# Four message-passing layers in one program: stage borders, edge attributes and the encoder-decoder data flow rearranged

## The reference

```python
h = jnp.maximum(_layernorm(x, axis=-1), 0.0)
x = x + _L0_gnn_ref(h, edge_index, ...)      # normalised sums over sources, then one matmul
h = jnp.maximum(_layernorm(x, axis=-1), 0.0)
x = x + _L1_gnn_ref(h, ..., edge_type_8)     # one of 8 matrices per edge, sums over targets
h = jnp.maximum(_layernorm(x, axis=-1), 0.0)
x = x + _L2_gnn_ref(h, edge_index, ...)      # encoder 128->128->64, decoder 64->128->128
h = jnp.maximum(_layernorm(x, axis=-1), 0.0)
x = x + _L3_gnn_ref(h, edge_attr_32, ...)    # attention over edges, needs efeats @ a_e
```

## Time and profile before

| | us |
|---|---|
| median of 2 runs | 7244.42 (7242.15 to 7246.7) |
| the profiled execution | 7248.66 |
| its span, first to last instruction | 7246.9 |

### The profile page before, as it was taken

How to read it: one execution, slowest core, us unless ns; L and a number is a source line. 1 busy time by engine, 2 the same in 40 slices (tenths; PEclk the granted TensorE clock), 3 DMA queues, 4 the chain that set the end, 5 groups by cost and what they waited for, 6 DMA issues and landing times. The chain is left out here.

```text
span 7246.9 us, 107353 instructions
## 1 busy us (share of the span) xinstructions
PE 3460.2 (48%) x18429; PEld 2590.8 (36%) x18429; DVE 4887.1 (67%) x19215; ACT 2860.8 (39%) x7124; POOL 4935.2 (68%) x4572
## 2 busy tenths in 40 slices
PE   7655366556668888820027776001884333333000
PEld 1111255546667777720015555001663222222000
DVE  7999688876778888878867776223773455555544
ACT  0366211118863333346656665000331355554222
POOL 0377578884557777777767750777887677775677
PEclk9755599998989999965568888555997555555555
DMA  7488678779973333357779997223995333332443
GB/s 298 150 293 293 186 136 144 142 120 323 340 224 97 97 94 97 94 150 196 197 261 378 374 348 236 52 52 109 349 342 181 100 102 102 102 102 82 135 135 113
DMA packets 1168584, 1327.05 MB, mean 183 GB/s; under 512 B 231276, under 2 KB 968790, under 8 KB 1157939
## 3 DMA queue, kind: packets, MB, share of 16 engines
q1 hardware_dynamic: 961680, 1002.76, 42.6%
q0 software_dynamic: 206768, 323.00, 18.7%
HBM read 706.30 MB, written 646.54 MB: 187 GB/s over the span
## 5 line engine op out<-in xcount | busy, mean ns | idle before, releaser
L1807 PE MATMUL ps<-dense,w 128*128 128x256 f32 x3136 | 731.3, 386 | 146.1 <-DVE dense L1537 145.2
L555 POOL DMA_INDIRECT t_src<-tot,sidx x392 | 621.5, 1585 | 182.6 <-issue 90.2
L1807 PEld LDWEIGHTS ps<-dense,w 128*128 128x128 f32 x3136 | 581.6, 190 | 263.6 <-DVE dense L1537 162.3
L715 POOL DMA_INDIRECT dense<-t_y,ends_i x392 | 372.9, 951 | 329.4 <-ACTq L453 210.2
L1731 PE MATMUL ps<-oneh_c,oneh_p 128*128 128x395 f16 x1568 | 458.8, 430 | 279.4 <-DVE oneh_c L890 270.3
L785 ACT ACTIVATE estd<-emv,epsc 128x2 f32<-128x2 f32 (+1 forms) x588 | 174.1, 296 | 943.8 <-DVE emv L768 943.8
L678 POOL DMA_INDIRECT t_yacc<-dense,keyg x392 | 462.3, 1179 | 121.9 <-issue 117.3
L1537 DVE SCALAR_TENSOR_TENSOR dense<-xT,ps 128x256 f32<-128x256 f32 x1568 | 537.1, 415 | 4.5 <-ACT xT L1990 3.4
L653 POOL DMA_INDIRECT out_rows<-dense,keyi x392 | 392.1, 1000 | 182.9 <-DVE dense L1713 108.8
L715 POOL DMA_INDIRECT dense<-t_xs,ends_i x392 | 378.3, 965 | 152.2 <-issue 130.4
L1207 POOL DMA_INDIRECT dense<-out_rows,ends_i x392 | 394.7, 1007 | 121.6 <-issue 121.0
(11 more groups left out here) (323 smaller groups left out, 11842.4 us busy)
## 6 DMA issues: line engine op xcount, KB each, us to landing
dense<-t_xs SPq DMA_DIRECT2D x78, 1320.0 KB
dense<-in_x SPq DMA_DIRECT2D x156, 640.0 KB
t_xs<-dense SPq DMA_DIRECT2D x98, 528.0 KB
t_xs<-hb SPq DMA_DIRECT2D x78, 660.0 KB
t_src<-dense SPq DMA_DIRECT2D x99, 512.0 KB, 6.3
t_sum<-dense SPq DMA_DIRECT2D x98, 512.0 KB
t_src<-dense SPq DMA_DIRECT2D x78, 640.0 KB
dense<-t_src SPq DMA_DIRECT2D x78, 640.0 KB
```

The lines of the kernel that those rows point to most:

```text
L555: gp.indirect_dma_start(t_src, bass.IndirectOffsetOnAxis(ap=sidx[:, p.k, c:c + 1], axis=0), tot[:, p.k, c, :], None, compute_op=ALU.add).t ...
L715: gp.indirect_dma_start(rows[:, p.k, c, :], None, table, bass.IndirectOffsetOnAxis(ap=index[:, p.q * 2 + c:p.q * 2 + c + 1], axis=0)) \
L1807: i = nc.tensor.matmul(ps[:, o:o + 2 * P], w1[:, k, :], xm[:, p.w, k, :], start=(k == 0), stop=(k == R - 1))
```

## The change

1. **Borders.** A new `leave_phase` counts up the gate without waiting. At the end of the layernorm stage, VectorE, TensorE and ScalarE use it (SP and GpSimd still wait); at the end of the third layer's edges, all five engines do.
2. **First sums.** The run ends are computed before that border. The attributes, their products and loads are moved to the stage of the second edges, with `a_e` copied to PSUM by ScalarE; in that stage every sixth pair, from pair 2 on, carries a part.
3. **First convolution.** SP issues the first six loads of `x` at the end of the first sums.
4. **Encoder.** SP loads the first three blocks during the edge stage ahead of it. `y` is stored with lag 7 instead of 6. L801, L813, L1596 and L1612 go (the square of the norm is made once for all blocks, epsilon goes in as the root's bias); two one-column memsets come in.
5. **The last 37 blocks (42 to 78)**: the joined `x` is not stored. The decoder loads both halves from `t_xs` and adds them on VectorE ahead of the bias. The decoder's `x` tile now has the layout of `t_xs` for all blocks, so the load from `t_x` of the first 42 lands in rows of 512 bytes that do not adjoin. Tiles of these stages move in `dense` to make room.

```diff
+LATE = 14 * SLOTS
+def is_late(b):
+    return b >= LATE if isinstance(b, int) else second_part[0]
...
+        def leave_phase(eng, who):
+            phases[who] += 1
+            eng.drain().then_inc(gate, 1)
...
             pair_loop(sp, (rest_of_rows, 0), (clear_sums, 0))
+            for u in (4, 5, 0, 1, 2, 3):
+                sp.wait_ge(E0["mm"].sem, E0["mm"].after(NPAIR - (NPAIR - 1 - u) % RING))
+                sp.dma_start(xin0[u], rows_of(x, u, P)).then_inc(X0["load"][u].sem, 16)
...
+            def enc_ahead(p):
+                if isinstance(p.q, int) and p.q in (6, 8, 10):
+                    u = (p.q - 6) // 2
+                    rows = PT if u == 0 else P
+                    sp.dma_start(xs[u][0:rows], rows_of(t_xs, NB - u, rows)).then_inc(L2["ld"][u].sem, 16)
...
             def enc_load(r, u, p):
...
-                if needed(r):
+                if needed(r) and not is_late(b - SLOTS):
...
             def enc_store_x(r, u, p):
                 b = r * SLOTS + u
+                if is_late(b):
+                    return
...
-            node_loop_back(sp, (enc_load, 0), (enc_store_x, 1), (enc_store, 6), (enc_sums, 1))
+            node_loop_parts(sp, (enc_load, 0), (enc_store_x, 1), (enc_store, 7), (enc_sums, 1))
...
             def dec_load(r, u, p):
...
-                sp.dma_start(xin[u][0:p], rows_of(t_x, NB - b, p)).then_inc(L3["ld"][u].sem, 16)
+                if is_late(b):
+                    sp.dma_start(x3[u][0:p], rows_of(t_xs, NB - b, p)).then_inc(L3["ld"][u].sem, 16)
+                else:
+                    sp.dma_start(x3_own[u][0:p], rows_of(t_x, NB - b, p)).then_inc(L3["ld"][u].sem, 16)
...
             def e3_sums(p):
+                if p.q == 2:
+                    v.wait_ge(AE["row"].sem, AE["row"].after(1))
+                if p.q % 6 == 2 and p.q < 8 * 6:
+                    attributes(p.q // 12, p.q // 6 % 2)
...
             def dec_bias(r, u, p):
                 v.wait_ge(L3["ld"][u].sem, L3["ld"][u].after(r * 16 + 16))
+                if is_late(r * SLOTS + u):
+                    nc.vector.tensor_tensor(x3_own[u][0:p], x3_own[u][0:p], x3_sums[u][0:p], ALU.add) \
+                        .then_inc(L3["joined"].sem, 1)
```

More of the change, by code:

```diff
@@ L131, in node_loop_back, with node_loop_parts, at, loop @@
                 fn(r - back if back else r, u - lag + back * SLOTS, P)
+    for b in range(NB, NB + 1 + most):
+        at(b)
+LATE = 14 * SLOTS
+second_part = [False]
+def is_late(b):
+    return b >= LATE if isinstance(b, int) else second_part[0]
+def node_loop_parts(eng, *stages):
+    most = max(lag for _, lag in stages)
+    peeled = (SLOTS + most + SLOTS - 1) // SLOTS
+    middle = (most + SLOTS - 1) // SLOTS
+    def at(b):
+        for fn, lag in stages:
+            if 0 <= b - lag <= NB:
+                fn((b - lag) // SLOTS, (b - lag) % SLOTS, PT if b == lag else P)
+    def loop(lo, hi):
+        with eng.Fori(lo, hi) as r:
+            for u in range(SLOTS):
+                for fn, lag in stages:
+                    back = (lag - u + SLOTS - 1) // SLOTS if lag > u else 0
+                    fn(r - back if back else r, u - lag + back * SLOTS, P)
+    for b in range(peeled * SLOTS):
+        at(b)
+    second_part[0] = False
+    loop(peeled, LATE // SLOTS)
+    for b in range(LATE, LATE + middle * SLOTS):
+        at(b)
+    second_part[0] = True
+    loop(LATE // SLOTS + middle, NB // SLOTS)
     for b in range(NB, NB + 1 + most):
@@ L1421, in keys_late @@
                 vec.tensor_tensor(firsti[:, 0:1], nextf[:, 2:3], nextf[:, 3:4], ALU.min)
+            nc.vector.memset(se[:, :], 0.0)
+            nc.vector.memset(cont[:, 0:1], 0.0)
+            nc.vector.memset(keyend[:, T - 1:T], float(2 * NR))
+            nc.vector.tensor_tensor(cont[:, 1:T], dst_f[:, 1:T], dst_f[:, 0:T - 1], ALU.is_equal).then_inc(C0["made"].sem, 1)
+            v.wait_ge(C0["made"].sem, C0["made"].after(1))
+            chain(nc.vector.scalar_tensor_tensor(out=keyend[:, 0:T - 1], in0=cont[:, 1:T], scalar=float(2 * NR),
+                                                 in1=dst_f[:, 0:T - 1], op0=ALU.mult, op1=ALU.add))
+            keys_late()
+            ln_vector(v, A0, dis[0])
+            leave_phase(v, VE)
             def needs():
@@ L1435, in e0_between @@
             def e0_between(pair):
-                if isinstance(pair.q, int) and pair.q == 0:
-                    nc.vector.memset(se[:, :], 0.0)
-                    nc.vector.memset(cont[:, 0:1], 0.0)
-                    nc.vector.memset(keyend[:, T - 1:T], float(2 * NR))
-                    nc.vector.tensor_tensor(cont[:, 1:T], dst_f[:, 1:T], dst_f[:, 0:T - 1], ALU.is_equal) \
-                        .then_inc(C0["made"].sem, 1)
-                    v.wait_ge(C0["made"].sem, C0["made"].after(1))
-                    nc.vector.scalar_tensor_tensor(out=keyend[:, 0:T - 1], in0=cont[:, 1:T], scalar=float(2 * NR),
-                                                   in1=dst_f[:, 0:T - 1], op0=ALU.mult, op1=ALU.add)
-                if isinstance(pair.q, int) and pair.q == 1:
-                    keys_late()
                 if isinstance(pair.q, int) and pair.q == 8:
                     needs()
-                if isinstance(pair.q, int) and 3 <= pair.q < 7:
-                    attributes(pair.q - 3)
             nc.vector.tensor_tensor(aside.rearrange("p (q c) -> p q c", c=4),
@@ L1586, in enc_stats @@
                 v.wait_ge(L2["join"].sem, L2["join"].after(b + 1))
-                stats(v, L2, b, u, p, x2[u], dis[1], NB - b)
+                for k in range(K):
+                    i = nc.vector.bn_stats(st[0:p, k, :], x2[u][0:p, k, :])
+                i.then_inc(L2["bn"].sem, 1)
+                v.wait_ge(L2["bn"].sem, L2["bn"].after(b + 1))
+                nc.vector.memset(carried[:, 0:1], 0.0)
+                for k in range(K):
+                    i = nc.vector.bn_aggr(mv[0:p, k, :], st[0:p, k, :])
+                i.then_inc(L2["mv"].sem, 1)
             def enc_h_scales(r, u, p):
@@ L1756, in _ @@
             node_loop(pe, (target_count, 0))
-            end_phase(pe, PE)
+            leave_phase(pe, PE)
             sums_tensor(pe)
@@ L1932, in _ @@
             ln_scalar(a, A0)
-            end_phase(a, AC)
+            leave_phase(a, AC)
             def e0_keys(p):
```

158 lines of the change are left out of this document (89 added, 69 removed).

## The result

The changed kernel takes 7142.7 us (7142.3 to 7143.1, two runs) against 7244.42, 102 us or 1.4% less. The ratio on record is 0.9853, with a 95% interval from 0.9832 to 0.9874; the quotient of the two medians, 0.9860, lies within it. The profiled execution took 7143.1 us with a span of 7141.4, 105.5 less than the span before.

| | forecast | measured |
|---|---|---|
| first sums (to the convolution's first block) | -48 | -37.3 |
| first convolution | -5 | -2.0 |
| relational layer, third layer's edges | 0 | 0.0 |
| encoder, start (to block 6) | -10 | -5.6 |
| encoder, blocks 6 to 41 | -13 | -9.4 |

The account below looks back on a forecast made before the run. GpSimd's scatters were taken to pace first sums and decoder, DMA and SP's order the encoder. Terms -48 + 2 - 5 - 10 - 13 - 67 + 27 = -114 gave 7134.7 profiled, 7130 median; range 7075 to 7185 us.

Parts of the forecast that it names:

- the likeliest case: Whole kernel: the forecast itself, 7130 us, own range 7095 to 7165, chance 0.62.
- First sums: First sums: without run ends and attributes, 3.75 us per pair holds from the first pair; -48 us, between -42 and -53.
- 5 between 0 and 11.8: First convolution: six loads of `x` leave a DMA-bound stage; 5 us gained, at most 11.8.
- Second edges: Second edges: moved products fit into VectorE's idle time, loads share the DMA engines; +2 us, +9 if half shows.
- with six pairs of lead I take 2: Second edges: GpSimd gathers six pairs ahead, so the added parts mostly hide; +2 us.
- Encoder, start and early blocks: Encoder: three blocks loaded ahead, -10 us at the start; later store of `y`, -13 us in blocks 6 to 41.
- Late blocks: Encoder, blocks 42 to 77: without the store of `x`, 7.8 us per block for 9.65; -67 us.
- The first rival: Encoder's late blocks: transfers rule there too, 9.0 us instead of 7.8; +43 us, 7173 us, chance 0.13.
- the second (SP's order alone): Encoder: SP's order alone set the pace; blocks 6 to 41 at 7.8 us too, 54 us less, 7076, chance 0.14.
- Decoder: Decoder: 37 joins on VectorE hold GpSimd's scatters, 0.73 us each; +27 us, transfers 0.
- The third rival: Decoder: each join holds GpSimd for its whole length; 55 us for 27, 7158 us, chance 0.09.
- Decoder's blocks as the bound: Decoder, a rival: SP's ring makes a late block cost 14.6 us; +192 us, 7322 us, chance 0.02.

Follow-up runs that it names:

- the four kernels show: Changed kernel (ratio 0.9853) and three edits of it: `y` at lag 6, 0.9931; `x` stored for all blocks, 0.9896; both, 0.9946.
- the mean of five: Five profiles with the changed kernel's decoder unchanged: mean scatters of 1.210 to 1.232 us, decoder 644.5 to 652.3 us.
- the loads spread: Changed kernel with the second edges' attribute loads in four parts behind the run-sum stores of pairs 4, 24, 44 and 64: ratio 0.9831.

## Why the prediction was right, point by point

The total came out at 7142.7 for 7130, within the likeliest case's own range, and by its mechanism: the gain lies in the first sums and above all in the late encoder blocks, and the decoder gives some back. The terms were less exact than the sum; too much gain in the first sums and too little loss in the second edges stand against too small a gain in the late blocks and too large a loss in the decoder. So the mechanism was right, and that the sum came so near is in part luck.

- **First sums**, -48 for -37.3. The term itself was nearly right: the first ten pairs took 44.3 us for 90.0, where I had 42.5, and from the gate to the first scatter it was 5.5 us, as I had it, for 6.6 before; that is 46.8 us. What I had put at nothing is the rest. The last 16 pairs got 3.4 us longer, under the loads of `x` that the change puts there. The gate came 1.6 us later, and so did GpSimd's first gather of the layernorm stage already (285.09 us for 283.46); the convolution began 1.0 us later behind the last scatter; the pairs between took 3.5 us more. (Over all profiles these pairs vary by 9 us, and in the nine with this stage as in the changed kernel the convolution begins 34 to 45 us earlier than in the one profile before.) The loads of `x` I had costed in the convolution alone, at "5 between 0 and 11.8": they were worth 2.0 there, and nothing by the run without them. How much of the gain belongs to the run ends and how much to the attributes was not run apart; the waits show that the two together held GpSimd.
- **Second edges**, +2 for +8.4. The step that failed is "with six pairs of lead I take 2". I had set GpSimd's lead against VectorE's products, and four of the six did hide. The loads did not: they stand ahead of the first run-sum stores, which free VectorE's ring, and they slow the first gathers' landing, so that the first two products showed as well. The end that I had named, +9 for half of the loads showing, was the nearer.
- **Encoder, start and early blocks**, -10 and -13 for -5.6 and -9.4. Right in kind: the early blocks stayed with the transfers. Blocks 6 to 41 took 351.3 us for 360.7; the five other profiles with lag 7 and 37 late blocks have 345.1 to 350.1, around the 13 that I had. The three loads ahead were costed at their gain only; the edge stage that they were taken into lost 3.9 us between its first and last gather.
- **Late blocks**, -67 for -75.7. VectorE is late next, as said, at 7.55 us for the 7.8 that I took. The first rival (transfers rule here too, 9.0 us) is excluded by 7.55; the second (SP's order alone) by lag 7 with `x` stored, 9.75 beside GpSimd. My account of two limits, of which each hides the other, is what the four kernels show.
- **Decoder**, +27 for +16.2. The step that failed is "it stands directly ahead of the bias add, which leaves GpSimd less to run in between, so I take 0.73". It is the other way round: directly ahead of the bias add the join takes over most of that add's hold. Without it the scatters were 1.8 us shorter than in the changed kernel, and 3.3 shorter than the mean of five; so 0.05 to 0.1 us a join. The 0.73 thus failed by far, and the loss came from what I had put at nothing. The other 12 to 14 us I cannot settle: the bias adds alone held scatters for 56 to 68 us in the four kernels without joins, and which part of that is the new layout, the double load or the meeting of two rhythms was not told apart. One profile each points to the first two: with the new layout alone (`x` stored for all blocks) the decoder took 638.1 and 640.0 us for 632.7 before, with the double load but no join 645.7, with both 648.9; but profiles of one and the same decoder lie 8 us apart. The third rival (55 us) is excluded.

The Trainium skill (SBUF — State Buffer, "Terms") has the loser of the shared port pair blocked, not slowed. I had weighed that against 83 us of loss beside 245 us of such operations and found that the trace did not agree. For GpSimd it does: each held scatter waits for the operation's very end. Only scatters that start during it are held, and for what is left of it; that makes a third, and not the whole. For VectorE it does not: in the changed kernel no scatter under way holds such an operation back (1.47 to 1.57 us for all 78 full bias adds).

- **Decoder's blocks as the bound**: no. The last result came 20 us behind the last scatter, with 37 joins as with none.

## What to carry to other kernels

Where two limits coincide, removing either shows little, and a test of one edit alone would have called both useless: cost them as a pair. A load that is moved to where an engine is idle still goes through queues in which other, smaller transfers wait; look for the first small store behind it and for who waits for that. A GpSimd stream beside VectorE is slowed by operations with two SBUF inputs by where they start and end. Taking such an operation off VectorE brought 30 us of decoder here; putting two back to back showed in the holds, but not surely in the time.

## What the runs showed of the hardware that was not expected

Scatters of the decoder over 1.02 us, all but one at most in each profile, have one cause and one size: they end 0.85 us behind the end of a VectorE operation with two SBUF inputs. A scatter that is already under way when such an operation starts is not lengthened (at most 1.02 us for 78 of 79 in the changed kernel; the one left, near the decoder's start, took 3.55 us, and each profile has one such). VectorE's bias adds are not lengthened by scatters (1.47 to 1.57 us).

The same product of 3136 elements per partition held a scatter for 4.56 us with its vector in SBUF and held no gather with the vector in PSUM. With the loads spread, all four products of 3.42 us had whole gathers of GpSimd of 0.95 us beside them. These are gathers, where the 4.56 us was a scatter; but gathers are held as well: in the attention scores of the changed kernel 105 of 392 (L1281) took over 1.05 us, up to 1.21, and every one of them starts beside a VectorE operation with two SBUF inputs (L1761). The Trainium skill (SBUF — State Buffer, "Who interferes with whom") says that a VectorE instruction with one SBUF input at most, outside its 2-port modes, does not contend with GpSimd; the trace agrees, with these 0.95 us.

An encoder whose VectorE rules keeps its pace exactly: 7.55 us a block in the ten kernels that have late blocks at lag 7, from the first of them or soon after to the last, with GpSimd's writes beside it or without them.
